# Transposing the probabilities of a query tile three steps behind its scores, not two

## The reference

```
x = x + 0.5 * ffn(layernorm(x))
x = x + attn(layernorm(x))
x = x + 0.5 * ffn(layernorm(x))

attn: q, k, v = x @ wq, x @ wk, x @ wv          per head
      q, k = rope(q) / sqrt(128), rope(k)
      probs = softmax(where(causal, q @ k.T, -1e30))
      attn = (probs @ v) @ wo                   summed over heads
```

## Time and profile before

| what | value |
|---|---|
| median of 3 runs | 1544.28 us |
| profiled execution | 1547.47 us, span 1545.7 us |
| PE busy | 1450.9 us, 94% |
| DVE busy | 1148.4 us, 74% |
| ACT busy | 945.3 us, 61% |
| POOL busy | 807.8 us, 52% |
| a unit in the middle (541.57 to 571.47) | 29.90 us |

### The profile page before, as it was taken

The page is one execution under the profiler, slowest core; times in us unless marked ns, Lnnn a source line. Parts: engine busy times, 40 slices in busy tenths (PEclk is TensorE's granted clock), DMA queues, the critical chain, the costliest instruction groups (busy, mean ns, idle before and its releaser), DMA issues.

```text
span 1545.7 us, 26680 instructions
## 1 busy us (share of the span) xinstructions
PE 1450.9 (94%) x8992; PEld 1280.4 (83%) x8992; DVE 1148.4 (74%) x2536; ACT 945.3 (61%) x1951; POOL 807.8 (52%) x735
## 2 busy tenths in 40 slices
PE   5799999789999999999999999999999976999998
PEld 4578777679899899989989998998999865877776
DVE  7678878877776777777677767767767776787787
ACT  4444444577776777677677767767767644444443
POOL 4546345355556555555555555555555543633644
PEclk9899999999999999999999999999999998999999
DMA  4000000200000000000000000000000020000000
GB/s 164 1 0 1 1 0 0 68 8 8 15 8 8 15 8 8 15 1 15 15 1 8 21 1 8 22 1 8 8 1 1 9 102 0 1 15 0 14 14 14
DMA packets 10822, 23.55 MB, mean 15 GB/s; under 512 B 848, under 2 KB 4944, under 8 KB 10576
## 3 DMA queue, kind: packets, MB, share of 16 engines
q1 hardware_dynamic: 10704, 22.04, 4.2%
HBM read 19.94 MB, written 2.10 MB: 14 GB/s over the span
## 4 chain that ended last, share of the span: by engine, by line
PE 78%; DVE 12%; issue 5%; POOL 2%; ACT 1%; DVEq 0%; DMA 0%; POOLq 0%; ACTq 0%
PE ps L1184 23%; PE ps L1186 22%; PE ps L1185 22%; PE ps L1475 9%; DVE ps L1114 2%; DVE up_act L971 1%; DVE pT_l L310 1%; POOL w_l L310 1%; DVE hid L981 1%; DVE hid L986 1%; DVE x_sb L915 1%; DVE xn L836 1%; DVE base_gate L956 1%; ACT up_act L661 0%; DVE stats L817 0%
## 5 line engine op out<-in xcount | busy, mean ns | idle before, releaser
L582 POOL TENSOR_SCALAR probs<-probs,inv_sum 128x128 f32<-128x128 f32 (+7 forms) x256 | 210.6, 823 | 390.8 <-DVE inv_sum L1070 390.7
L1114 DVE CUSTOM_DVE_ANT_0 ps<-ps,causal 128x128 f32<-128x128 f32 (+7 forms) x256 | 195.1, 762 | 217.6 <-PE ps L1186 216.0
L764 ACT ACTIVATE probs<-ps,neg_max 128x128 f32<-128x128 f32 (+7 forms) x256 | 189.3, 740 | 76.2 <-DVE neg_max L1114 76.2
L310 DVE TENSOR_TENSOR pT_l<-ps,pT_h 128x512 fp32r<-128x512 f32 (+3 forms) x384 | 200.8, 550 | 2.1 <-ACT pT_h L743 1.9
L743 ACT ACTIVATE pT_h<-ps 128x512 fp32r<-128x512 f32 (+3 forms) x384 | 174.1, 490 | 37.6 <-PE ps L1475 35.1
L571 POOL TENSOR_TENSOR rot_sin<-swapped,rope 128x512 f32<-128x512 f32 x128 | 165.0, 1289 | 55.5 <-ACT swapped L720 52.5
L1475 PE MATMUL ps<-ident,probs 128*128 128x128 f32 x1152 | 169.8, 274 | 23.3 <-DVE pT_l L310 20.4
L1184 PE MATMUL ps<-pT_h,v_h 128*128 128x256 f32 x640 | 181.1, 283 | 0.8 <-DVE oA_l L310 0.8
L1186 PE MATMUL ps<-pT_h,v_l 128*128 128x256 f32 x640 | 180.9, 283 | 0.0
L1185 PE MATMUL ps<-pT_l,v_h 128*128 128x256 f32 x640 | 180.6, 282 | 0.0
L310 POOL TENSOR_TENSOR hid_l<-hid,hid_h 128x512 fp32r<-128x512 f32 (+1 forms) x88 | 114.1, 1297 | 98.1 <-ACT hid_h L663 98.1
(11 more groups left out here) (185 smaller groups left out, 4336.4 us busy)
## 6 DMA issues: line engine op xcount, KB each, us to landing
w_raw<-attn_w SPq DMA_DIRECT2D x32, 256.0 KB, 2.6
w_in<-ffn_w SPq DMA_DIRECT2D x10, 744.0 KB, 9.1
x_sb<-x_in SPq DMA_DIRECT2D x4, 512.0 KB, 5.4
out<-x_sb SPq DMA_DIRECT2D x4, 512.0 KB, 2.9
rope<-rope_w SPq DMA_DIRECT2D x1, 1024.0 KB, 7.9
expand_raw<-expand_w SPq DMA_DIRECT2D x2, 384.0 KB, 12.4
```

The costliest lines, as they stand in the source:

```text
L310: return eng.tensor_tensor(dst, src, high.bitcast(F32), ALU.subtract)
L582: pool.tensor_scalar(probs[s % 4][:, 0:n], probs[s % 4][:, 0:n], inv_sum[:, s % 4:s % 4 + 1], 1.0, ALU.mult, ALU.mult).then_inc(probs_read ...
L764: act.activation(probs[t % 4][:, 0:a * n].rearrange("p (a n) -> p a n", a=a), view, ACT.Exp, bias=neg_max[:, t % 4:t % 4 + 1], scale=-1.0, ...
L1114: dve.tensor_tensor_reduce(out=view, in0=view, in1=causal[:, SEQ - a * n:].rearrange("p (a n) -> p a n", a=a), scale=-SCALE, scalar=HUGE, ...
```

## The change

One constant:

```
-T_LAG, PV_LAG, OUT_LAG = 2, 5, 8
+T_LAG, PV_LAG, OUT_LAG = 3, 5, 8
```

## The result

The changed kernel takes 1562.36 us (median of 5, 1560.27 to 1564.65) against 1544.28: a ratio of 1.0117, with a 95% interval of 1.0105 to 1.0128. I had forecast 1544.6 and a range up to 1554. In the profiled executions the span went from 1545.7 to 1562.9 us, so 17.2 us are to be found.

A forecast was written before the change was run, and what follows sets the result against it. TensorE, busy for 94% of the span, bounds the kernel. Steady part 0 (15 output units at -0.10, 15 value units at +0.10), start -0.8, end +1.1: +0.3 on 1544.28, so 1544.6 us; range 1537 to 1554.

The forecast's parts named there:

- The new stop of step 3: Step 3, both units: TensorE's turn of tile 0 waits for VectorE's first low of tile 7; 0.39 us lost per unit.
- the gain of step 7: Step 7: TensorE's stop for VectorE's low shrinks; 0.49 us gained in an output unit, 0.29 in a value unit.
- the longer VectorE step 3: VectorE work queued behind step 3's lows comes 0.8 us later in output units; costed at nothing.
- the steps 0, 2, 4, 5 and 6: Steps keeping their slack: one transpose fewer each, except seven more in step 2; no new stop.
- bank of step 7: Rival, output units: VectorE's longer step 3 delays the swap freeing the output's bank; +5 us, 1550; chance 0.16.
- The step that failed: Step 1: its wait for a 4-block low behind a short maximum stays as before; no added cost.
- The rival of the late high copy: Step 3: ScalarE's high copy comes behind other work, so the first low starts late; +16 us, 1561; chance 0.08.
- Start: First unit: turns stop waiting for GpSimd, values still wait for step 4's swap, next unit starts at 331.48, not 332.24; -0.8 us.
- the clock as a rival of every unit: Clock falls behind the new stops, 3.6 us at 0.53 in each of 31 units; +50 us; chance 0.03.
- End: Last unit, without side work: 1.84 us stop at step 3, six more transposes behind the last scores, other stops gone; +1.1 us.
- The rule on the clock: TensorE: frequent short idles from cycling PSUM banks can swing the clock, making two stops a unit worse; weighed, not priced in.

The follow-up runs named there:

- all three edits: Changed kernel with the swap of step 0 one step later and the turns of steps 3 and 7 each behind the next scores: 1529.41 us, ratio 0.9902.
- the kernel with two: Changed kernel with the swap of step 0 one step later and the turn of step 3 behind the scores of step 4: 1534.69 us, ratio 0.9940.

## Why the prediction was wrong

**What held.** The new stop of step 3 (0.39 forecast; step 3 at 2.66 to 2.67 where 2.63 was forecast), the gain of step 7 in output units (3.76 forecast, 3.78 measured) and in value units, the longer VectorE step 3 that costs nothing, and the steps 0, 2, 4, 5 and 6 (in value units step 6 is 0.12 longer than forecast and step 7 0.15 shorter). No bank of step 7 came late in output units, so that rival is out.

**The step that failed** is a sentence that priced an edit at nothing: "step 1 already waited for a 4-block low behind a short maximum, and still does". It looked at VectorE's queue only, and took the low's other input, ScalarE's high copy, as early. In the kernel before the copy was on time with next to nothing to spare in output units and 0.3 to 0.4 us in value units, and it hung, through the swap and the cosines, on the end of the last values, not on TensorE's turns. I had worked out just such a chain for the bank of step 7, and moved it with TensorE's own start. Here the same question was not asked. Measured cost: 0.66 and 0.28 a unit, 14.1 us; the moved swap takes it away.

**The reason behind it** is the sum itself. It took stops one by one: minus 0.49 here, plus 0.39 there. The stop of step 7 was also the cover of the chain that ends in step 1, and taking it away could only pay if that chain had slack. The run with the covered step 7 shows the exchange without the rest of the change: 0.36 gained, 0.37 given back.

**The rival of the late high copy** had the right mechanism (a low that waits for ScalarE, whose copy stands behind other work), a price close to the result (+16, 1561) and the wrong step. It was put in step 3, where the copy of tile 7 is early, and so got 0.08. That its price fits is luck: it was 0.55 in each of 30 units, and what the runs show is 0.66 and 0.28 in another step, and 2.7 us more than forecast at the start and the end.

**Start: +0.6 where -0.8 was forecast.** The values of the first unit's step 5 start at 321.96, as forecast (322.10 before), but TensorE had stood still for 2.31 us ahead of them, where before it had waited twice, 0.96 us for the scaled probabilities and 0.88 for the swap. Behind it the granted clock fell. The row of the values and a stretch behind them in the changed kernel, then the first of the two waits and the same stretch in the kernel before (the stretch: length, busy per engine, clock):

```profile
321.96 0.39 PE L1184 MATMUL ps<-wv_h,xnT_h 128*128 128x256 f32 x1 [2.31 <-ACT swapped L720]
...
323.00:326.40 3.40, 3.40 (x15) 3.18 (x14) 1.29 (x2) 2.19 (x5) 2.28 (x3) 0.50 0.00 0
```

```profile
319.61 0.55 PE L1475 MATMUL ps<-ident,probs 128*128 128x128 f32 x3 [0.96 <-POOL probs L582]
...
323.00:326.40 3.40, 3.40 (x22) 3.04 (x21) 2.09 (x4) 2.36 (x5) 2.44 (x3) 1.00 0.03 5
```

In the stretch at 0.50 TensorE got through 15 instructions instead of 22. I had the clock as a rival of every unit, and not of the start. That the fall makes the whole 1.4 us of difference is argued from these rows, and not tried.

**End: +2.4 where +1.1 was forecast.** The stop of step 3 was forecast at 1.84 with its restart, and shows 1.59 of modelled idle. What I had missed is a stop in step 0, where one of 0.23 stood:

```profile
1246.55 0.85 PE L1475 MATMUL ps<-ident,probs 128*128 128x128 f32 x6 [0.71 <-DVE pT_l L310]
...
1255.87 0.30 PE L1475 MATMUL ps<-ident,probs 128*128 128x128 f32 x1 [1.59 <-DVE pT_l L310]
```

The last unit took 1.05 us longer up to its last scores (20.51 after 19.46), and what follows them 1.4. So the account is 14.1 for step 1, 1.4 for the start, 1.3 for the end, and the 0.3 that had been forecast: 17.1 of 17.2 us.

**The rule on the clock.** Over the 62 stops between 326.4 and 1250, about two a unit, the clock of the changed kernel stays at 1.00. The rule of the Trainium skill that the prediction weighed (TensorE: Matmul & The Clock Gate, "A second HAM failure mode: psum-queue depth-cycling"), that frequent short idles can make the clock swing, isn't borne out by these stops. Whether it holds where they stand closer together stays open: in two of the four kernels made from the changed one the clock fell once in the last unit, behind short stops (rows in the last section).

## What to carry to other kernels

A stop of the bounding engine can be the cover of a chain on the other engines that doesn't start from that engine's next instruction. Before a stop is booked as gained, follow what the next few waits hang on back to an event that won't move, and compare the lengths: no wait in the trace can mean no slack. And where an instruction has two inputs, price both; the one that isn't named as the releaser may be just behind. Then look in the in-order queue of each supplier for work that could stand behind the urgent copy instead of ahead of it: here that move is worth nothing alone, 13 us after one change and about 4 after another.

## What the runs showed of the hardware

In the changed kernel the granted clock fell to 0.50 (the level of 1.2 GHz) 1.0 us after TensorE had gone on from a stop of 2.3 us, and was 0.50 from 323.0 to 326.4 us. Between 320 and 324 us it was 0.87 on average in the changed kernel, and 0.57, 0.77, 0.61 and 0.70 in the four made from it, whose longest stops there were 2.4 to 3.2 us. It was 1.00 there in the kernel before and in the four made from it, whose wait for the same swap is 0.9 us.

In the middle of the program stops of up to 1.3 us left it at 1.00. In the last unit, where TensorE has less to do, the same two stops, 0.71 and 1.33 us, had two outcomes. With the moved swap (the stretch's last figures are the clock, the DMA share and GB/s):

```profile
1232.47 0.84 PE L1479 MATMUL ps<-ident,probs 128*128 128x128 f32 x6 [0.71 <-DVE pT_l L310]
1235.00 1.60 PE L1479 MATMUL ps<-ident,probs 128*128 128x128 f32 x7 [1.33 <-DVE pT_l L310]
...
1235.20:1238.50 3.30, 3.30 (x16) 3.30 (x15) 1.56 (x9) 1.22 (x3) 0.26 (x1) 0.50 0.71 211
```

In the changed kernel the first of them is the row at 1246.55 above; the second and the stretch behind it:

```profile
1249.08 0.95 PE L1475 MATMUL ps<-ident,probs 128*128 128x128 f32 x7 [1.33 <-DVE pT_l L310]
...
1249.00:1252.50 3.50, 3.42 (x28) 3.45 (x29) 2.84 (x13) 1.65 (x4) 0.54 (x2) 1.00 0.65 201
```

The last unit of the profiled execution with the moved swap took 22.11 us up to its last scores, against 20.51, and steps 1 and 2, where the clock was low, make up the difference (7.76 against 6.18). In the kernel before with its turn of step 7 moved, a stop of 2.1 us in the last unit left the clock at 1.00:

```profile
1246.39 0.85 PE L1476 MATMUL ps<-ident,probs 128*128 128x128 f32 x6 [2.13 <-DVE pT_l L310]
```

The two stops of 0.71 and 1.33 us also left it at 1.00 in the two kernels with the covered step 3 of which one has the moved swap too. With all three edits it fell in the last unit again, to 0.50 from 1236.4 to 1239.7 us, behind a stop of 1.6 us, and the same stop left it at 1.00 in the kernel with two. So the stops by themselves don't tell whether the clock falls; what does is not shown here.
